# Four-layer image network on one NeuronCore: one scaled identity per state index for both channel halves, POOL units' decays in SBUF, 1024-wide silu and softplus, and an order planned over all instructions

## The chip, the core and the metric

The kernel runs on one core of a Trainium2 chip. The metric is the device time of one execution in microseconds (us). The engines are called PE (TensorE), DVE (VectorE), ACT (ScalarE), POOL (GpSimd) and SP (SyncE, which here only issues DMAs).

## The reference, cut to what matters

Thirty-two images of 128 channels and 32x32 pixels (1024 tokens) go through four layers, each with a group norm ahead of it and an addition behind it: a 3x3 convolution, a selective scan (Mamba) over the tokens in four directions, a coordinate attention with two small scans, and a simulated four-qubit circuit. Nearly all the time goes into the second:

```python
uc = silu(conv1d(u)); dt = softplus(dtr @ dt_proj_w.T + dt_proj_b); A = -exp(A_log)
def step(h, inp):                      # for each token, d in 256 channels, n in 16 states
    dA = exp(dt_t[..., None] * A)
    h = dA * h + (dt_t * u_t)[..., None] * B_t[:, None, :]
    y = einsum('bdn,bn->bd', h, C_t)
y = (ys + uc * Dp) * silu(z)           # v0..v3: as is, channels flipped, tokens flipped, both
```

## The kernel before, in words

For each image the second layer is cut into 128 **units**: 4 directions `d` x 2 channel halves `h` x 16 state indices `n`. Sixteen units in a row with one `d` and `h` are a pass. A unit works on 128 channels x 1024 tokens in f32:

- ACT computes its decay exp(dt * A_n) (L1160).
- Its input du * B_n (du is dt * u) is made in one of three ways, by the letter of the unit in the table `KINDS` (L48). **D**: PE spreads the row B_n over the partitions into a PSUM slot (L1659), DVE multiplies by du (L1455). **P**: a DMA of SP reads the row B_n from HBM, broadcast to 128 partitions, into `b_rows` (L861), and POOL multiplies (L966) into the unit's ring slot in SBUF. **Z**: ACT scales the turned (tokens by channels) du by B_n, one 128x128 chunk at a time (`zmul`, L1069), and PE turns the result back into a PSUM slot (`turn_z`, L1662).
- DVE runs the scan along the tokens (L1469) into the slot `u % 8` of `ring`. One operand of each scan is in PSUM: for D and Z the input, with the decay in the ring; for P the decay, with the input in the ring.
- For each pair of units POOL multiplies both ring slots at once by the broadcast rows C_n (L983, the "product"), which another DMA has brought into `c_rows` (L867).
- PE turns each product and adds it into `y_acc` in PSUM (`add_y`, L1667), which frees the ring slot. A P unit's input may be written once the unit 8 back has been added.

All other work (the norms, the convolutions, the projections, the last two layers of the image before, the front of the image after) is a list of `step`s that the planner `lay` (L468) puts between the units on each engine by costs, due times and a table of shifts, `SHIFTS`. In the program before, the units' own instructions keep a fixed order on each engine (`unit_programs`, L363), and side steps are inserted at places of it. On POOL that order is: inputs of the P units of the next pair, then the product of this pair. Each engine runs its instructions in order.

SP issues the row loads in one in-order queue, `load_pair(k)` (L851) for k = 0, 1, 2, ...: the B rows of the P units of pair k, each once the buffer is free, and then the C rows of pair k, once the product `CB_BUFS` pairs back is done:

```python
for u in (2 * k, 2 * k + 1):
    if kind_of(u) == "P":
        if j >= B_BUFS: sp.wait_ge(pool_input, j - B_BUFS + 1)
        sp.dma_start(b_rows[:, j % B_BUFS, :], ...)
sp.wait_ge(prod_ready, s * PAIRS + k - CB_BUFS + 1)
sp.dma_start(c_rows[:, b, :, :], ...)
```

With `CB_BUFS` = 4 the B rows of pair k stand behind the C rows of pair k-1, which wait for the product of pair k-5.

Of the kernel before, what the change touches and what calls it, by code (L numbers as in the profile page):

```python
# [35 lines left out]
BANK = 512  # L36
# [7 lines left out]
PASSES = DIRS * HALVES  # L44
UNITS = PASSES * NST
# [70 lines left out]

def norm(tag, after=()):
    b = ("norm", tag)
    return [step(("moment", tag, 0), "A", None, after), step(("moment", tag, 1), "A"), step(("group_mean", tag), "P", b),
            step(("group_neg", tag), "A", b), step(("group_eps", tag), "D", b), step(("group_rstd", tag), "G"),  # L120
            step(("group_shift", tag), "A"), step(("norm", tag), "A")]
# [15 lines left out]
def silu_pair(of, d, h, name, parts, after=()):  # L137

    key = lambda c: (of, d, h, c)
    steps = []  # L140
    for c in range(2):
        for k in parts:
            steps += [step((name, d, h, *k, c), "P", key(c), after if not steps else [])]
    return steps + [step(("silu", of, d, h, c), "A", key(c)) for c in range(2)]


def operands(d, first=False):

    steps = []
    for h in range(HALVES):  # L150
        steps += silu_pair("u", d, h, "conv_in", [(k,) for k in range(TAPS)])
    if d % 2:
        for h in range(HALVES):
            taken = [] if first and d == 1 else [("take", 2 + h if d == 3 else "before")]
            steps += silu_pair("z", d, h, "z", [()], taken)
# [8 lines left out]
def timestep(d, h):  # L164

    steps = []
    for c in range(2):
        b = ("dt", d, h, c)
        parts = [("part", d, 2, c)] if (d, h) != (0, 1) else []
        steps += [step(("dt_proj", d, h, c), "P", b, parts)]  # L170
        steps += [step((k, d, h, c), e, b) for k, e in (("dt_soft", "A"), ("dt_copy", "A"), ("dt_u", "D"))]
    return steps


def turn_du(d, h, last=None):

    steps = []
    for c in range(2):
        b = ("turn_du", d, h, c)
        after = [] if c or last is None else [("zmul", last, 1)]  # L180
        steps += [step(("turn_du", d, h, c), "P", b, after), step(("turned_du", d, h, c), "A", b)]
    return steps if "Z" in KINDS[HALVES * d + h] else []
# [11 lines left out]
def mix():  # L194

    steps = [step(("take", "before"), "D", None, [("sum", -1)])] + turn_y("before", 1, 1)
# [55 lines left out]
def set_up():  # L252
# [11 lines left out]
    for f in range(2):  # L264
        for h in range(HALVES):
# [13 lines left out]
SIDE_COST = {"conv_in": .9, "xproj": .9, "z": 1., "dt_proj": .42, "mix": .9, "conv0": .9, "nin": 1., "adjust": .9,  # L279
             "turn_y": .5, "turn_du": .5, "turned_du": .6, "turn_b": .6, "turned_b": .3, "zmul": 1.35, "rest": .3, "dtproj2": .9, "in2": 2., "spread2": .95, "mask2": 3.4, "xproj2": .9, "out2": .9, "unitary": .5,  # L280
             "post": 1.8, "group_mean": .7, "angles": 1.8, "gates": .5, "mlp1": .5, "mlp2": .5, "turn": .3, "squeeze": .3,
             "silu": .68, "cb_rows": .6, "part": .6, "dt_soft": .66, "dtsoft2": .3, "dtw": .3,
             "dt_copy": .6, "dt_u": .7, "turned_y": .6, "h1": .8, "relu2": .8,
             "squeeze_gelu": .4, "silu2": .8, "mlp_gelu": .3, "sine": .6, "decay2": .6, "moment": 1.25, "group_neg": .45, "group_shift": .25, "norm": 1.25,
             "add0": .75, "keep0": .9, "keep1": .9, "keep2": .9, "keep3": .9, "add1": .7, "over": .5, "over_copy": .6, "sums": 3.5, "taps2": 1.7, "tapsum2": 1.05, "dta2": 1.1, "input2": .7,
             "scan2": 1.25, "prod2": .7, "ysum2": 1.05, "outer_h": 1.25, "outer_w": 1.25, "times_x": .7, "add2": .7,
# [1516 lines left out]
```

## Time and profile before

| | us |
|---|---|
| median of 3 runs (13699.96 to 13713.61) | 13713.5 |
| the profiled execution | 13695.55 |
| its span in the trace | 13693.8 |

Line numbers below are those of the kernel before. In the rows "busy" is the time that an engine executes, "idle before, releaser" is the time that it stood still just ahead of an instruction and what ended it. "From issue to landing" is the time of a DMA from the start of its issue on SP until its data is there. PE records are doubled for f32 operands of a true matmul (two records a chunk), and not for turns.

### The profile page before, as it was taken

The page shows a single profiled execution, that of the slowest core. Times are in us where ns is not written, and L with a number is a line of the kernel's source. Part 1 is how long each engine was busy: PE and PEld are TensorE (multiplying, and loading weights), DVE is VectorE, ACT ScalarE, POOL GpSimd, SP SyncE. Part 2 cuts the span into 40 slices and gives each one's busy share as a digit, 9 for nine tenths or more (in the row PEclk, how much of TensorE's full clock was granted, in tenths as well). Part 3 has the DMA queues.
Part 4 walks back from the last instruction along what each step waited for, and adds up shares of the span by engine and source line. Part 5 has one row for each costly group of instructions (what it writes and reads, how often), then busy time and mean ns, then how long its engine had stood idle before and what let it go on. Part 6 is the DMA issues. An engine that isn't in the chain of part 4 may idle for free.

```text
span 13693.8 us, 182039 instructions
## 1 busy us (share of the span) xinstructions
PE 11889.6 (87%) x67228; PEld 8271.3 (60%) x67228; DVE 12477.9 (91%) x8406; ACT 11898.3 (87%) x18047; POOL 13045.4 (95%) x3978
## 2 busy tenths in 40 slices
PE   7888888888888888888888888888888888888886
PEld 4566666666666666566666566665666666666654
DVE  7899999999999999999999999999999999999985
ACT  6888888888888888888888888888888888888884
POOL 7999999999999999999999999999999999999995
PEclk8999999999999999999999999999999999999997
DMA  5566566656566666566665665655666656666552
GB/s 191 224 226 228 228 224 230 235 224 229 221 235 232 228 228 226 226 230 233 226 230 221 233 231 226 230 226 226 234 230 225 230 223 230 233 227 228 226 213 115
DMA packets 544698, 3067.83 MB, mean 224 GB/s; under 512 B 60378, under 2 KB 60474, under 8 KB 281538
## 3 DMA queue, kind: packets, MB, share of 16 engines
q1 hardware_dynamic: 543810, 3056.18, 59.1%
q8 instruction: 534, 8.75, 0.3%
q14 instruction: 354, 2.90, 0.1%
HBM read 2990.40 MB, written 48.76 MB: 222 GB/s over the span
## 4 chain that ended last, share of the span: by engine, by line
POOL 33%; PE 22%; issue 16%; ACT 13%; DVE 9%; DMA 4%; POOLq 0%; DVEq 0%; SPq 0%; ACTq 0%
POOL ring L983 24%; PE work L1481 10%; POOL ring L966 8%; PE y_acc L1496 7%; DVE ring L1469 6%; ACT ring L1160 3%; ACT L1000 3%; DMA cb_rows_scratch<-stack 2%; PE y_acc L1481 2%; DVE slot L1455 2%; PE slot L1496 1%; DMA b_rows<-cb_rows_scratch 1%; PE slot L1481 1%; ACT slot L1160 1%; ACT z_t L1069 1%
## 5 line engine op out<-in xcount | busy, mean ns | idle before, releaser
L983 POOL TENSOR_TENSOR ring<-ring,c_rows 128x2048 f32<-128x2048 f32 x2048 | 9297.0, 4548 | 392.6 <-DVE ring L1469 375.4
L1469 DVE TENSOR_TENSOR_SCAN ring<-ring,slot 128x1024 f32<-128x1024 f32 x2560 | 5817.8, 2280 | 218.7 <-PE slot L1496 82.3
L1496 PE MATMUL y_acc<-wk,ring 128*128 128x128 f32 x32768 | 4513.7, 284 | 671.7 <-POOL ring L983 656.5
L1496 PEld LDWEIGHTS y_acc<-wk,ring 128*128 128x128 f32 x32768 | 3984.0, 147 | 1506.1 <-POOL ring L983 850.8
L1469 DVE TENSOR_TENSOR_SCAN ring<-slot,ring 128x1024 f32<-128x1024 f32 x1536 | 3495.0, 2276 | 370.4 <-POOL ring L966 266.4
L966 POOL TENSOR_TENSOR ring<-du,b_rows 128x1024 f32<-128x1024 f32 x1536 | 3634.2, 2369 | 64.7 <-DMA b_rows<-cb_rows_scratch 53.3
L1160 ACT ACTIVATE ring<-dt,a_neg 128x1024 f32<-128x1024 f32 x2560 | 2846.2, 1139 | 19.6 <-PE y_acc L1496 9.8
L1000 ACT ACT_TABLE_LOAD x1883 | 2415.9, 1283 | 33.7
L1455 DVE TENSOR_TENSOR slot<-du,slot 128x1024 f32<-128x1024 f32 x1856 | 2246.1, 1210 | 73.5 <-PE slot L1481 71.4
L1481 PE MATMUL work<-h_new,fused 128*128 128x512 f32 x4096 | 1936.5, 603 | 8.6 <-DVE padded L1334 3.1
L1160 ACT ACTIVATE slot<-dt,a_neg 128x1024 f32<-128x1024 f32 x1536 | 1707.1, 1113 | 240.6 <-DVE ring L1469 230.6
L1069 ACT ACTIVATE z_t<-du_t,b_t 128x128 f32<-128x128 f32 x5632 | 1792.2, 389 | 33.0 <-PE slot L1496 10.2
L1481 PE MATMUL slot<-stack,sel 96*128 96x512 bf16 x3712 | 1200.5, 407 | 291.6 <-DVE ring L1469 284.2
L1481 PEld LDWEIGHTS work<-h_new,fused 128*128 128x128 f32 x4096 | 735.1, 193 | 630.5 <-issue 591.6
L1481 PE MATMUL work<-padded,wk 128*128 128x512 f32 (+1 forms) x1792 | 927.5, 622 | 53.0 <-ACT u_conv L1039 31.9
L1496 PE MATMUL slot<-wk,z_t 128*128 128x128 f32 x5632 | 778.4, 282 | 193.4 <-DVE ring L1469 176.3
L1496 PEld LDWEIGHTS slot<-wk,z_t 128*128 128x128 f32 x5632 | 648.1, 144 | 455.2 <-issue 372.8
L1481 PEld LDWEIGHTS slot<-stack,sel 96*128 96x128 bf16 x3712 | 320.3, 102 | 861.6 <-DVE ring L1469 506.8
L1050 ACT ACTIVATE stack<-work 32x512 bf16<-32x512 f32 x768 | 448.3, 584 | 313.7 <-PE work L1481 299.8
L1481 PE MATMUL work<-u_conv,wk 128*125 128x512 f32 x1024 | 515.0, 620 | 24.0 <-ACT yz L1078 20.6
L1481 PEld LDWEIGHTS y_acc<-diag_d,u_conv 128*128 128x128 f32 x4096 | 494.9, 192 | 60.3 <-issue 33.0
L1481 PE MATMUL y_acc<-diag_d,u_conv 128*128 128x128 f32 x4096 | 508.1, 277 | 0.0
(178 smaller groups left out, 9934.9 us busy)
## 6 DMA issues: line engine op xcount, KB each, us to landing
c_rows<-cb_rows_scratch SPq DMA_DIRECT2D x2048, 1024.0 KB, 4.7
b_rows<-cb_rows_scratch SPq DMA_DIRECT2D x1536, 512.0 KB, 5.6
x_next<-in_x SPq DMA_DIRECT2D x32, 512.0 KB, 5.6
x_new_scratch<-x_next SPq DMA_DIRECT2D x32, 512.0 KB, 7.8
h_old<-h_new SPq DMA_DIRECT2D x32, 512.0 KB, 7.9
x_old<-x_new_scratch SPq DMA_DIRECT2D x32, 512.0 KB, 10.1
out<-x_old SPq DMA_DIRECT2D x32, 512.0 KB, 7.9
cb_rows_scratch<-stack SPq DMA_DIRECT2D x128, 116.0 KB
```

Of the source, the lines that this page charges most:

```text
L966: pool.tensor_tensor(ring[:, u % RING, :], du[:, h, :], b_rows[:, j % B_BUFS, :], ALU.mult).then_inc(pool_input, 1)
L983: pool.tensor_tensor(pair, pair, c_rows[:, k % CB_BUFS, :, :], ALU.mult).then_inc(prod_ready, 1)
L1000: act.preload_act_table_set(name)
L1050: ins = act.activation(half(stack[r, d % 2, :], c), w[r, :], ACT.Copy)
L1069: ins = act.activation(z_t[:, turned % Z_BUFS, j * P:(j + 1) * P], du_t[:, j * P:(j + 1) * P], ACT.Copy, scale=b_t[:, d % 2, j * NST + n:j ...
L1160: act.activation(slot, dt[:, h, :], ACT.Exp, scale=a_neg[:, h * NST + n:h * NST + n + 1]).then_inc(decay_ready, 1)
L1455: dve.tensor_tensor(operand[u % 2], du[:, h, :], operand[u % 2], MUL).then_inc(input_ready, 1)
L1469: dve.tensor_tensor_scan(slot, a, b, 0.0, MUL, ADD).then_inc(scan_done, 1)
L1481: return pe.matmul(out_ap, w, x, start=start, stop=stop, skip_group_check=True)
L1496: ins = pe.matmul(chunk(out_t, j), chunk(x, j), kc("ident"), is_transpose=True, start=start and j % (BANK // P) == 0, stop=stop, skip_grou ...
```

## The change

`KINDS` has 58 D, 44 P and 26 Z units an image in place of 58, 48 and 22, and every Z stands at the same `n` in both halves of a direction. ACT now scales the **identity** by B_n once for both halves (13 times 8 chunks an image in place of 22 times 8), and `turn_z` is a true f32 matmul of du_t by that scaled identity. P units' decays go to `decays` in SBUF, so both operands of a P scan are in SBUF, and PSUM slots alternate over D and Z units alone. Silu, softplus, the copy of dt and dt * u take both banks at once (1024 wide). The halves are ordered 0, 1, 1, 0, 0, 1, 1, 0, so that `y_acc` carries over two passes at two places of an image: two takes and two identity additions fewer. Row sums for three of the four norms come from the additions' accumulators. `CB_BUFS` and `B_BUFS` go from 4 to 3. ACT issues the stores of the C and B rows. The planner orders all instructions of all engines itself, with other costs and a new `SHIFTS`; like the planner before, it has no term for the row loads except behind a store.

```diff
-KINDS = ('DPDPZDDDDPZPDPDZ', 'DPDZDPDZDPZPDPDP', 'DDDDDPZPDPPPZDDP', 'DPDPDPZZPPZZDPDP',
-         'DPZPPDPZDPPDZPDP', 'DDDPDPDDPDZZDDPD', 'DPDPDZZPDDDPDZDP', 'DPDPDPZDDPDPZPDP')
+KINDS = ('DPDPDZZDDPPZZDDP', 'DPDPDZZDPDPZZDDP', 'DPPDDPPDZDZDZDZP', 'DPDPDDDPZPZDZDZP',
+         'DPDZZPPDDDPPZDPP', 'DDPZZDDDPDPPZPDP', 'DPDDZDDPDPPDDZDP', 'DDDPZPPDPDPDDZDP')
-CB_BUFS = 4
-B_BUFS = 4
-Z_BUFS = 2
+CB_BUFS = 3
+B_BUFS = 3
+Z_BUFS = 4
+DECAY_BUFS = 2
...
-    (-413, 123, -1143, -1629, -1503, -1060, -1344, -1469, -1469, -2434, -2294, -1545, -1418, -1624, -1701, -489,
...
+def unit_flows(kind):
+    of = lambda *kinds: [u for u in range(UNITS) if kind_of(u) in kinds]
+    return {"D": [[("b", u) for u in of("D")], [("scan", u) for u in range(UNITS)]],
+            "G": [[("input", u) for u in of("P")], [("prod", u) for u in range(1, UNITS, 2)]],
...
     if k == "input":
-        return [(("sum", u - RING), 0)] * (u >= RING) + [(("dt_u", d, h, 1), 0)] * (u >= NST and first_of("P", u)) + rows
+        return [(("sum", u - RING), 0)] * (u >= RING) + [(("dt_u", d, h), 0)] * (u >= NST and first_of("P", u)) + rows
...
-                if k >= CB_BUFS or s > 0:
-                    sp.wait_ge(prod_ready, s * PAIRS + k - CB_BUFS + 1)
+                if loads >= CB_BUFS:
+                    sp.wait_ge(prod_ready, loads - CB_BUFS + 1)
...
-                    for j in range(4 * i, 4 * i + 4):
-                        ins = act.activation(z_t[:, turned % Z_BUFS, j * P:(j + 1) * P], du_t[:, j * P:(j + 1) * P], ACT.Copy,
-                                             scale=b_t[:, d % 2, j * NST + n:j * NST + n + 1])
+                    for j in range(CH // Z_STEPS * i, CH // Z_STEPS * (i + 1)):
+                        ins = act.activation(z_t[:, tile_of(u), j * P:(j + 1) * P], kc("ident"), ACT.Copy,
+                                             scale=b_turned(d, s)[:, j * NST + n:j * NST + n + 1])
...
-                        slot = operand[u % 2]
-                        if u >= 2 or s > 0:
-                            act.wait_ge(scan_done, s * UNITS + u - 1)
+                        slot = decays[:, (s * N_P + number("P", u)) % DECAY_BUFS, :]
...
-                    turn(operand[u % 2], z_t[:, (s * N_Z + number("Z", u)) % Z_BUFS, :], True, True).then_inc(z_turned, 1)
+                    for j in range(CH):
+                        ins = mm(chunk(slot_of(u, s), j), chunk(du_t, j), chunk(z_t[:, tile_of(u), :], j),
+                                 j % (BANK // P) == 0, True)
```

**POOL, the start of a middle image** (units 1, 3, 9, ... are P; `b_rows` rows are inputs, `c_rows` rows are products of pairs). Before:

```order
L966 TENSOR_TENSOR ring<-du,b_rows 128x1024 x2
L983 TENSOR_TENSOR ring<-ring,c_rows 128x2048 x3
L966 TENSOR_TENSOR ring<-du,b_rows 128x1024
L983 TENSOR_TENSOR ring<-ring,c_rows 128x2048
L966 TENSOR_TENSOR ring<-du,b_rows 128x1024
```

and now:

```order
L1100 TENSOR_TENSOR ring<-du,b_rows 128x1024 x2
L1109 TENSOR_TENSOR ring<-ring,c_rows 128x2048
L1100 TENSOR_TENSOR ring<-du,b_rows 128x1024
L1109 TENSOR_TENSOR ring<-ring,c_rows 128x2048 x2
L1100 TENSOR_TENSOR ring<-du,b_rows 128x1024
```

The input of unit 9, in pair 4, stood behind the products of pairs 0, 1 and 2, and stands behind that of pair 0 now. Counted over a middle image: before, 47 of 48 inputs had three products between the one that releases their B row and themselves, and one had four; now 7 of 44 inputs come behind that product with no other between, 24 have one between, 10 have two, and 3 have three.

**SP, the same place** (row loads with the semaphores that they wait for). Before:

```order
L861 DMA b_rows<-cb_rows_scratch 128x1024 [waits pool_input]
L867 DMA c_rows<-cb_rows_scratch 128x2048 [waits prod_ready] x3
L861 DMA b_rows<-cb_rows_scratch 128x1024 [waits pool_input]
L867 DMA c_rows<-cb_rows_scratch 128x2048 [waits prod_ready]
L861 DMA b_rows<-cb_rows_scratch 128x1024 [waits pool_input]
```

and now:

```order
L1004 DMA b_rows<-cb_rows_scratch 128x1024 [waits pool_input]
L1010 DMA c_rows<-cb_rows_scratch 128x2048 [waits prod_ready] x3
L1004 DMA b_rows<-cb_rows_scratch 128x1024 [waits pool_input]
L1010 DMA c_rows<-cb_rows_scratch 128x2048 [waits prod_ready]
L1004 DMA b_rows<-cb_rows_scratch 128x1024 [waits pool_input]
```

The queue reads the same: the B row of unit 9 stands behind the C rows of pairs 1 to 3. What moved is the product that the last of these waits for: with 4 buffers it was the last of the image before, with 3 it is that of pair 0.

## Rows read from the trace of the kernel before

**Rows 1.** The page's first lines: span, busy time of each engine.

```profile
span 13693.8 us, 182039 instructions
PE 11889.6 (87%) x67228; PEld 8271.3 (60%) x67228; DVE 12477.9 (91%) x8406; ACT 11898.3 (87%) x18047; POOL 13045.4 (95%) x3978
```

**Rows 2.** A window of 419 us in the middle: engines' busy us, PEclk, DMA share, GB/s.

```profile
1940.30:2359.30 419.00, 367.77 (x2105) 255.57 (x2104) 391.24 (x260) 372.97 (x567) 408.50 (x127) 0.96 0.62 229
```

**Rows 3.** An instruction that POOL runs once an image, from 1600 to 13100 us.

```profile
L929 POOL TENSOR_TENSOR m<-m x27: 444/450/503, 1940.3 to 12833.9; 128x128 f32<-128x128 f32 x27
```

**Rows 4.** POOL's waits in those 26 images: us in total, times, longest.

```profile
POOL ring L983 <- DVE ring L1469: 263.0, 259, 2.7
```

**Rows 5.** The costliest groups of POOL: busy us, mean ns, idle before and releaser.

```profile
L983 POOL TENSOR_TENSOR ring<-ring,c_rows 128x2048 f32<-128x2048 f32 x2048 | 9297.0, 4548 | 392.6 <-DVE ring L1469 375.4
L966 POOL TENSOR_TENSOR ring<-du,b_rows 128x1024 f32<-128x1024 f32 x1536 | 3634.2, 2369 | 64.7 <-DMA b_rows<-cb_rows_scratch 53.3
```

**Rows 6.** Timeline of POOL: start us, us.

```profile
13477.04 4.53 POOL L983 TENSOR_TENSOR ring<-ring,c_rows 128x2048 f32<-128x2048 f32 x1
13481.52 2.37 POOL L966 TENSOR_TENSOR ring<-du,b_rows 128x1024 f32<-128x1024 f32 x1
13483.84 4.54 POOL L983 TENSOR_TENSOR ring<-ring,c_rows 128x2048 f32<-128x2048 f32 x1
```

**Rows 7.** Timeline of POOL and SP's queue in the middle: start us, us.

```profile
5998.40 4.55 POOL L983 TENSOR_TENSOR ring<-ring,c_rows 128x2048 f32<-128x2048 f32 x1 [0.66 <-DVE ring L1469]
6002.99 0.32 SPq L867 DMA_DIRECT2D c_rows<-cb_rows_scratch  x1
6003.35 0.43 SPq L861 DMA_DIRECT2D b_rows<-cb_rows_scratch  x1
```

**Rows 8.** DMA issues, whole span, then two single loads: KB, median us to landing.

```profile
b_rows<-cb_rows_scratch SPq DMA_DIRECT2D x1536, 512.0 KB, 5.6
...
b_rows<-cb_rows_scratch SPq DMA_DIRECT2D x1, 512.0 KB, 5.1
...
b_rows<-cb_rows_scratch SPq DMA_DIRECT2D x1, 512.0 KB, 7.3
```

**Rows 9.** Timelines of SP and of POOL, the first image's first B row.

```profile
92.18 0.33 SPq L861 DMA_DIRECT2D b_rows<-cb_rows_scratch  x1
...
96.68 2.35 POOL L966 TENSOR_TENSOR ring<-du,b_rows 128x1024 f32<-128x1024 f32 x1 [50.35 <-DMA b_rows<-cb_rows_scratch]
```

**Rows 10.** Timeline of PE: a turn (x8), a true matmul of 8 chunks (x16).

```profile
6015.54 1.04 PE L1496 MATMUL slot<-wk,z_t 128*128 128x128 f32 x8
6016.42 1.13 PE L1481 MATMUL work<-wk,h_new 128*128 128x128 f32 x8
...
6041.58 1.95 PE L1481 MATMUL y_acc<-diag_d,u_conv 128*128 128x128 f32 x16
6043.36 1.04 PE L1496 MATMUL y_acc<-wk,ring 128*128 128x128 f32 x8
```

**Rows 11.** Groups of ACT, DVE and PE that the change touches: busy us, mean ns, idle.

```profile
L1000 ACT ACT_TABLE_LOAD x1883 | 2415.9, 1283 | 33.7
L1069 ACT ACTIVATE z_t<-du_t,b_t 128x128 f32<-128x128 f32 x5632 | 1792.2, 389 | 33.0 <-PE slot L1496 10.2
...
L1469 DVE TENSOR_TENSOR_SCAN ring<-slot,ring 128x1024 f32<-128x1024 f32 x1536 | 3495.0, 2276 | 370.4 <-POOL ring L966 266.4
...
L1282 DVE TENSOR_TENSOR du<-work,u_conv 128x512 f32<-128x512 f32 x512 | 346.9, 677 | 77.3 <-ACT dt L1058 77.3
L1286 DVE TENSOR_TENSOR yz<-y_acc,silu_z 128x1024 f32<-128x1024 f32 x128 | 155.2, 1213 | 149.9 <-PE y_acc L1496 149.4 <-ACT yz L1078 0.5
...
L1481 PE MATMUL y_acc<-yz,wk 128*128 128x512 f32 x512 | 247.3, 605 | 0.0
```

**Rows 12.** Timeline of the set-up: a POOL instruction over DVE's with two SBUF inputs.

```profile
14.23 0.55 POOL L925 TENSOR_TENSOR bnw<-bnw,neghalf 128x1 f32<-128x1 f32 x1 [11.51 <-DVE bnw L1214]
14.34 1.34 DVE L1188 SCALAR_TENSOR_TENSOR fused<-c_rows 128x256 f32<-128x256 f32 x3
```

More of the change, by code:

```diff
@@ L143, in silu_pair, with conv, gate_z, project @@
             steps += [step((name, d, h, *k, c), "P", key(c), after if not steps else [])]
-    return steps + [step(("silu", of, d, h, c), "A", key(c)) for c in range(2)]
-def operands(d, first=False):
-    steps = []
[L150 to L155, printed above, removed]
+    return steps + [step(("silu", of, d, h), "A", both(key(0), key(1)))]
+def conv(d, h):
+    return silu_pair("u", d, h, "conv_in", [(k,) for k in range(TAPS)])
+def gate_z(f, h, after=()):
+    return silu_pair("z", f, h, "z", [()], after)
+def project(d):
+    steps = []
     for c in range(2):
@@ L194, in mix @@
 def mix():
-    steps = [step(("take", "before"), "D", None, [("sum", -1)])] + turn_y("before", 1, 1)
+    steps = [step(("take", "before"), "D", None, [("sum", -1)])] + turn_y("before", 1, 0)
     for c in range(2):
@@ L276, in set_up @@
     return [[step(("zero",), "G")], weights, decays, scales, mixes, circuit]
[L279 to L286, printed above, removed]
-             "result": .75, "group_rstd": .55, "take": 1.2, "du2": .7, "zero": 2.5, "fuse": .43, "kron": 1.5, "gate": .17, "bn_rstd": .55, "m1": 2., "postw_mask": .35, "dterm2": .7, "dadd2": .7, "yz2": .7}
@@ L602, in image_streams @@
     takes = []
-    for p in range(PASSES - 1):
-        f, t, h = p // 4, p // 2 % 2, p % 2
-        after = [("sum", p * NST + NST - 1)]
-        if t == 0 and not first:
+    for p in TAKES:
+        f, h = p // 4, parts_of(p)[1]
+        after = [("sum", p * NST + NST - 1)] + ([("silu", "z", f, h)] if p % 4 else [])
+        if not first and p % 4 != 3:
             after += [(("post", 1) if h else ("angles",)) if f else ("mix", 4, 1)]
-        takes += [step(("take", p), "D" if t else "A", None, after)]
-        if t:
+        takes += [step(("take", p), "D" if p % 4 else "A", None, after)]
+        if p % 4:
             takes += turn_y("this", f, h)
@@ L635, in count @@
     def count(steps, e):
-        return sum(x[2] == e for x in steps)
+        return sum(x[1] == e and x[3] is not None for x in steps)
     def bases(kind, s):
@@ L647, in numbers @@
         n, out = dict.fromkeys("PADG", 0), {}
-        for x in steps:
-            n[x[2]] += 1
-            out[x[1]] = (x[2], n[x[2]])
+        for name, e, _, after in steps:
+            if after is not None:
+                n[e] += 1
+                out[name] = (e, n[e])
         return out
@@ L943, in step @@
                 ins.then_inc(side["G"], 1)
-            for _, name, e, _, after in before:
+            for name, e, _, after in before:
                 if e == "G":
@@ L986, in _ @@
             each_image(pool, image)
-            for _, name, e, _, after in finish:
+            for name, e, _, after in finish:
                 if e == "G":
@@ L1431, in _ @@
             dve.wait_ge(weights_in, 16 * 7)
-            for _, name, e, bank, after in before:
+            for name, e, bank, after in before:
                 if e == "D":
@@ L1633, in _ @@
             pe.wait_ge(weights_in, 16 * 7)
-            for _, name, e, bank, after in before:
+            for name, e, bank, after in before:
                 if e == "P":
@@ L1691, in image @@
-                side_steps(END["P"])
+                    turn(y_acc, ring[:, u % RING, :], starts, ends).then_inc(sum_done, 1)
+                for name, _, bank, after in order_of(plans[kind], "P"):
+                    if name[0] == "spread":
+                        spread_b(name[1])
+                    elif name[0] == "zturn":
+                        turn_z(name[1])
+                    elif name[0] == "sum":
+                        add_y(name[1])
+                    else:
+                        hold(pe, "P", base, of, after)
+                        step(name, image_of(name, s), bank_of[bank])
```

614 lines of the change are left out of this document (343 added, 271 removed), and 92 rows, old and new, of the table SHIFTS.

## The prediction

> **What bounds the kernel now.** I read the busy times first [rows 1]: POOL is busy for 95% of the span, DVE 91%, PE and ACT 87%. A window of one image in the middle says more [rows 2]: of 419.0 us POOL works 408.5, DVE 391.2, ACT 373.0, PE 367.8. That 419 us is the period: the instruction that POOL runs once an image goes from 1940.3 to 12833.9 us in 26 steps, which is 418.98 each [rows 3]. So POOL has 10.5 us to spare in an image. Its waits say what they are: 263.0 us in 26 images, 10.1 an image, go to products that wait for DVE's scans [rows 4]. Whatever changes POOL's time by x us an image changes the total by 32x; what the other engines save or pay counts only through a wait of POOL.
>
> POOL's work is 64 products and 48 inputs an image [rows 5]. By starts, a product takes 4.48 us and an input 2.32 [rows 6].
>
> **The change, part by part.**
>
> *Four P units fewer.* 4 x 2.32 = 9.3 us less POOL work an image. This is the whole gain on the engine that bounds.
>
> *Z units.* ACT scales 104 chunks an image in place of 176, at 1792.2 / 5632 = 0.318 us [rows 11]: -22.9 us of ACT. PE pays: a turn of 8 chunks takes 0.88 us from start to start, a true matmul of 8 chunks 1.78 [rows 10], so 22 x 0.88 becomes 26 x 1.78: +26.9. Two of four identity additions go: 247.3 / 32 / 2 = -3.9 [rows 11]. PE comes to 390.8 us an image, ACT to 350.
>
> *Wide silu, softplus, copy, dt * u; fewer table loads.* The program has 1471 table loads where there were 1883: 412 x 1.283 / 32 = -16.5 us of ACT [rows 11]. DVE's 512 half products of 0.677 us become 256; at 1.21 us, what the 1024-wide take takes [rows 11], that is -1.2 us. Both lie beside POOL's work and I cost them at nothing: the cover is POOL's period, and ACT and DVE stay under it.
>
> *Decays in SBUF, slots over D and Z alone.* DVE's scans of P units waited 266.4 us for POOL's inputs in all [rows 11]; scans that come sooner can only take from the 10.1 us of rows 4. In the other direction, both operands of 44 scans an image now come from SBUF. No scan of the trace does that. From below it costs nothing: the scan takes 2.276 us with the decay in PSUM. From above it costs POOL the whole scan, 44 x 2.28 = 100 us. I take nothing, since the one row that is near shows nothing, and keep the other end as a rival: in the set-up, POOL's L925 runs from 14.23 to 14.78, and DVE starts three instructions with two SBUF inputs at 14.34; they take 1.34 us, 0.45 each, with no gap, and POOL's is done in 0.55 [rows 12]. It reads one element a partition, so the row is weak.
>
> The Trainium skill, "SBUF — State Buffer", section "Who interferes with whom", speaks against this part: a DVE instruction with two SBUF inputs and a GpSimd one that reads SBUF exclude each other for the whole instruction. The rows of the set-up don't agree with it; by it the sum would be that of the second rival.
>
> *The B rows: three buffers and a free order.* Here the change loses what it wins. A P unit's B row is loaded behind the C rows of the pair before, in SP's one queue. With three C buffers those wait for the product of the pair four back. The row lands late: the product that starts at 5998.40 frees SP, which issues the C rows at 6002.99 and the B row at 6003.35 [rows 7], so 0.4 us after the product's end; the B row takes 5.6 us more by the median [rows 8]. The input can't start until 6.0 us after that product's end. Before, three products (13.4 us) lay between, and in the whole run POOL waited for B rows only at the start (53.3 us, rows 5). Now the order puts inputs up to there. I went through the 44 inputs of a middle image and added up the POOL work between the releasing product and the input: 2 inputs have nothing between (units 9 and 63), 4 have 2.3 us (another input), 9 have 4.5 us (a product), 2 have 5.0, and the rest 6.0 or more. The waits are 2 x 6.0 + 4 x 3.7 + 9 x 1.5 + 2 x 1.0 = 42.3 us; unit 38's row also waits for its buffer, freed 4.7 us before it is wanted, 0.9 more. A wait shelters the input behind it; walked through in order, with each wait moving all that follows, 39.6 us are left, in 18 inputs. The walk with 5.1 us from issue to landing, the quicker of the two single loads in rows 8, gives 31.6; with 6.0 it gives 46.4. The slower single load took 7.3, and a load into an idle queue, the first of all, 4.5 until POOL ran [rows 9], so no row shows one under 4.5.
>
> *What goes as POOL gets late.* The 10.1 us for scans: POOL now stands still 40 us an image elsewhere, and DVE, at 390 us of work, catches up meanwhile. All or none of it may go; I take 7, since the new waits are spread over the whole image but a scan also waits for a late input.
>
> *The stores from ACT, `x` loads, set-up and the last image's end* move by a few us in all: nothing.
>
> **The sum.** 419.0 - 9.3 + 39.6 - 7.0 = 442.3 us an image, 23.3 more than now; 32 x 23.3 = 746. On the profiled execution's 13695.6 that is 14441; the median of the runs shown lies 18 us higher, so 14460. PE at 390.8 and DVE at 390 have over 50 us to spare in that period. The ends: 419.0 - 9.3 + 31.6 - 10.5 = 430.8 gives 14090; 419.0 - 9.3 + 46.4 = 456.1 gives 14900.
>
> **The rivals.**
>
> *Faster: the loads are early enough.* If the B rows land before POOL wants them, only the first part is left: 419.0 - 9.3, and up to 5 us less waiting for scans, as ACT has 40 us less work and slots come free sooner. That is 13400 (13255 at best). It decides by the landing: at 4.1 us from issue, 4.5 from the product's end, the 9 inputs behind one product wait for nothing, 2 x 4.5 + 4 x 2.2 = 17.8 us are left, and with 9.3 and 7 off, the period is that of now. For it: the DMA engines are busy 62% of the time [rows 2], so a load might be quicker where the C rows ahead have landed. Against it: the C rows of 1 MB are issued 0.36 us ahead every time, and even the idle queue took 4.5. Chance 0.13, and 0.03 that it comes out within 0.2%, which is about what a measurement of this kernel can tell from no change.
>
> *Much slower: P scans and POOL exclude each other.* Each of the 44 scans of 2.28 us keeps POOL still, 100.3 us an image. Where it falls into POOL's waits for B rows it is free, so the period is between 442.3 + 100.3 - 39.6 = 503.0 and 542.6, and the time between 16400 and 17670, say 17000. For it: the kernel before has one operand in PSUM in every large DVE instruction beside POOL, even where ACT must write a second time for it. Against it: rows 12. It decides as soon as POOL and DVE can't both read; then products stretch beyond 4.54 us or P scans beyond 2.28. Chance 0.18.
>
> *The change doesn't do what it says* can't be on this engine: 1408 inputs are in the program where 1536 were.
>
> **How the numbers follow.** The forecast, 14460 with its own range of 14090 to 14900, has 0.64; the faster rival 0.13; no change 0.03; the exclusion 0.18; slower by another way, such as PE's sums freeing the ring too late at 390.8 us of work, 0.02. Slower by over 0.2% is then 0.84. The range must leave out no more than 0.2: it reaches from the faster rival, 13300, to 14900 and leaves the exclusion out.
>
> **What the profile would show.** POOL's inputs with B rows as what ended their wait, some 18 an image, 35 to 45 us an image in all, the longest near 6 us; POOL busy near 90%, with 1408 inputs of 2.37 us and products unchanged at 4.54; scans with both operands in SBUF at 2.28; the once-an-image instruction every 440 us; ACT under 80% of the span; B rows landing in 5 to 6 us. The forecast is wrong if POOL hardly waits for DMA, if a B row lands within 4.1 us of its issue, if the scans or products are longer than now, or if POOL waits for PE's sums instead.

## The result, and the profile after

The change takes 17046.0 us (median of 4 runs, 17015.5 to 17049.9) where the kernel before takes 13713.6: a ratio of 1.243, 95% interval 1.241 to 1.245. The forecast was 14460 and the range ended at 14900, so the time lies 2146 us beyond the range. It lies inside the second rival, the exclusion of P scans and POOL, which had 17000 and a chance of 0.18.

The page of the changed kernel, first lines (against [rows 1]), and a window of 533 us in its middle (against [rows 2]: the same columns, PE, PEld, DVE, ACT, POOL busy us, PEclk, DMA share, GB/s):

```profile
span 17045.9 us, 192114 instructions
PE 13574.0 (80%) x74844; PEld 9697.5 (57%) x74844; DVE 15134.9 (89%) x8150; ACT 10549.9 (62%) x14370; POOL 14465.0 (85%) x3850
```

```profile
6000.00:6533.00 533.00, 427.89 (x2379) 306.53 (x2379) 475.12 (x253) 339.12 (x463) 459.44 (x123) 0.90 0.48 178
```

POOL has 128 instructions fewer and is busy 1420 us longer; DVE has 256 fewer and is busy 2657 us longer. Both engines have fewer instructions, and those they have take longer. The groups say which (busy us, mean ns, idle before and releaser; against [rows 5] and [rows 11]):

```profile
L1109 POOL TENSOR_TENSOR ring<-ring,c_rows 128x2048 f32<-128x2048 f32 x2048 | 10198.4, 4992 | 802.6 <-DVE ring L1609 772.9 <-DMA b_rows<-cb_rows_scratch 18.1 <-PE y_acc L1645 11.5
L1609 DVE TENSOR_TENSOR_SCAN ring<-ring,slot 128x1024 f32<-128x1024 f32 x2688 | 6067.1, 2272 | 246.7 <-PE slot L1630 199.3 <-ACT ring L1299 18.9
L1609 DVE TENSOR_TENSOR_SCAN ring<-decays,ring 128x1024 f32<-128x1024 f32 x1408 | 5910.8, 4209 | 359.6 <-POOL ring L1100 358.7 <-issue 0.2
...
L1100 POOL TENSOR_TENSOR ring<-du,b_rows 128x1024 f32<-128x1024 f32 x1408 | 3951.7, 2812 | 1431.9 <-DMA b_rows<-cb_rows_scratch 1247.4 <-PE y_acc L1645 144.8 <-DVE ring L1609 38.1
...
L1134 ACT ACT_TABLE_LOAD x1470 | 1886.0, 1283 | 27.1
```

The scans with one input in a PSUM slot take 2.27 us, as before. Those with both in SBUF (`decays`, `ring`) take 4.21 us by the mean. POOL's product has gone from 4.548 to 4.992 us and its input from 2.369 to 2.812. The spread within a group is the better sign. This view of the tile `decays`, with minimum, median and maximum in ns, and that of an instruction which POOL runs once an image (0.45 us in [rows 3]) show it:

```profile
L1609 DVE TENSOR_TENSOR_SCAN ring<-decays,ring x1408: 2256/4274/6649, 101.6 to 16896.1; 128x1024 f32<-128x1024 f32 x176
```

```profile
L1068 POOL TENSOR_TENSOR m<-m x32: 452/2433/2445, 798.0 to 16962.7; 128x128 f32<-128x128 f32 x32
```

A scan takes between 2.26 us, its own time, and 6.65, its own time and most of a product's. The small POOL instruction takes 0.45 us or 2.43: 0.45 and most of a scan's 2.27. How one instruction comes to hold the other is read from the timeline of POOL and DVE at 6038 to 6062 us (start us, length us):

```profile
6037.98 4.53 POOL L1109 TENSOR_TENSOR ring<-ring,c_rows 128x2048 f32<-128x2048 f32 x1
...
6039.81 4.86 DVE L1609 TENSOR_TENSOR_SCAN ring<-decays,ring 128x1024 f32<-128x1024 f32 x1
6042.48 4.35 POOL L1100 TENSOR_TENSOR ring<-du,b_rows 128x1024 f32<-128x1024 f32 x1
6046.79 4.51 POOL L1109 TENSOR_TENSOR ring<-ring,c_rows 128x2048 f32<-128x2048 f32 x1
6046.83 2.27 DVE L1609 TENSOR_TENSOR_SCAN ring<-ring,slot 128x1024 f32<-128x1024 f32 x1
...
6053.60 4.54 POOL L1109 TENSOR_TENSOR ring<-ring,c_rows 128x2048 f32<-128x2048 f32 x1 [2.29 <-DVE ring L1609]
...
6056.88 3.40 DVE L1609 TENSOR_TENSOR_SCAN ring<-decays,ring 128x1024 f32<-128x1024 f32 x1
6058.09 2.44 POOL L1068 TENSOR_TENSOR m<-m 128x128 f32<-128x128 f32 x1
```

The product ends at 6042.51. The P scan starts at 6039.81, in the middle of it, and ends at 6044.67: that is 2.2 us, about one scan, after the product's end. The input starts at 6042.48 and ends at 6046.83, 2.2 us, about one input, after the scan's end. A product, a scan and an input stand one behind the other although two engines run them, and the wait is inside their durations; the views of waits don't list it. The next two lines are the control: a product and a scan with one input in a PSUM slot start together, at 6046.79 and 6046.83, and both take their own time, 4.51 and 2.27. The last three lines are like the first: product until 6058.14, scan until 6060.28, and only then the 0.45 us instruction, done at 6060.53.

The waits of POOL in 27 periods in the middle (us in total, times, longest; against [rows 4]):

```profile
POOL ring L1100 <- DMA b_rows<-cb_rows_scratch: 1068.6, 374, 8.3
POOL ring L1109 <- DVE ring L1609: 603.9, 310, 2.6
POOL ring L1100 <- PE y_acc L1645: 118.7, 97, 2.4
```

That is 39.6, 22.4 and 4.4 us an image. The once-an-image instruction runs from 1849.1 to 16042.2 us in 27 steps, a period of 525.7 where it was 419.0 [rows 3]. The period adds up: 64 products x 0.444 = 28.4 and 44 inputs x 0.443 = 19.5 longer; 39.6 for B rows; 12.3 more for scans; 4.4 for TensorE's sums; 2.0 in the small instruction; 9.3 less for four inputs: 96.9 of the 106.7. The rest was not added up.

### The profile page after: what moved, and what is told of

It reads as the page before. It is cut to its first block and busy times, and to the rows that moved or that the text cites. A ratio compares the mean times of both kernels' runs of the same rounds, so it can differ in the third digit from the quotient of the medians.

```text
span 17045.9 us, 192114 instructions
## 1 busy us (share of the span) xinstructions
PE 13574.0 (80%) x74844; PEld 9697.5 (57%) x74844; DVE 15134.9 (89%) x8150; ACT 10549.9 (62%) x14370; POOL 14465.0 (85%) x3850
## 5 line engine op out<-in xcount | busy, mean ns | idle before, releaser
L1109 POOL TENSOR_TENSOR ring<-ring,c_rows 128x2048 f32<-128x2048 f32 x2048 | 10198.4, 4992 | 802.6 <-DVE ring L1609 772.9
L1609 DVE TENSOR_TENSOR_SCAN ring<-ring,slot 128x1024 f32<-128x1024 f32 x2688 | 6067.1, 2272 | 246.7 <-PE slot L1630 199.3
L1609 DVE TENSOR_TENSOR_SCAN ring<-decays,ring 128x1024 f32<-128x1024 f32 x1408 | 5910.8, 4209 | 359.6 <-POOL ring L1100 358.7
L1100 POOL TENSOR_TENSOR ring<-du,b_rows 128x1024 f32<-128x1024 f32 x1408 | 3951.7, 2812 | 1431.9 <-DMA b_rows<-cb_rows_scratch 1247.4
L1299 ACT ACTIVATE decays<-dt,a_neg 128x1024 f32<-128x1024 f32 x1408 | 1602.6, 1142 | 1012.9 <-DVE ring L1609 1008.7
L1630 PEld LDWEIGHTS slot<-z_t,du_t 128*128 128x128 f32 x13312 | 1773.4, 213 | 472.2 <-issue 340.5
L1630 PE MATMUL slot<-z_t,du_t 128*128 128x128 f32 x13312 | 1863.0, 300 | 224.0 <-DVE ring L1609 217.7
L1206 ACT ACTIVATE z_t<-wk,b_t 128x128 f32<-128x128 f32 x3328 | 1144.9, 392 | 31.1
L1196 ACT ACTIVATE du_t<-work 128x512 f32<-128x512 f32 x512 | 304.3, 594 | 512.9 <-PE work L1645 509.4
L1630 PEld LDWEIGHTS work<-padded,wk 128*128 128x128 f32 (+1 forms) x1792 | 341.9, 210 | 410.1 <-issue 318.6
```

The costliest lines, as they stand in the source:

```text
L1100: pool.tensor_tensor(ring[:, u % RING, :], du[:, pass_of(d, h) % 2, :], b_rows[:, j % B_BUFS, :], ALU.mult).then_inc(pool_input, 1)
L1109: pool.tensor_tensor(pair, pair, c_rows[:, loads % CB_BUFS, :, :], ALU.mult).then_inc(prod_ready, 1)
L1196: ins = act.activation(half(du_t, c), w, ACT.Copy)
L1206: ins = act.activation(z_t[:, tile_of(u), j * P:(j + 1) * P], kc("ident"), ACT.Copy, scale=b_turned(d, s)[:, j * NST + n:j * NST + n + 1])
L1299: act.activation(slot, dt[:, pass_of(d, h) % 2, :], ACT.Exp, scale=a_neg[:, h * NST + n:h * NST + n + 1]).then_inc(decay_ready, 1)
L1609: dve.tensor_tensor_scan(slot, a, b, 0.0, MUL, ADD).then_inc(scan_done, 1)
```

## The experiments

Each kernel ran beside the kernel before on the same chip, which took 13698 to 13706 us by the median. "e3" and the like are the first letters of the labels. e1 has 4 runs, e7 has 10, e8 has 2, and e2, e3, e4, e5, e6 and e9 have one each; with one run, differences of less than some 40 us (0.3%) are not read.

**e1: the kernel before with three buffers of C rows.**

```diff
-CB_BUFS = 4
+CB_BUFS = 3
...
-                if k >= CB_BUFS or s > 0:
-                    sp.wait_ge(prod_ready, s * PAIRS + k - CB_BUFS + 1)
+                if loads >= CB_BUFS:
+                    sp.wait_ge(prod_ready, loads - CB_BUFS + 1)
```

The three buffers are counted on over the images, and three scratch places of the set-up move, since they lay in the fourth.

> The kernel before with three C buffers in place of four, its order unchanged. Both mechanisms' theory: each input still has two products (9 us) between the one that now releases its B row and itself, more than the 6.0 us that a row needs, so POOL waits for no B row and the time is that of before within 0.2%: 13685 to 13740. Rival (three buffers are too few by themselves, whatever the order): POOL waits for B or C rows, 2 us or more an image, over 13770.

Measured: 13792.0 us, ratio 1.0067 (1.005 to 1.0084), 93 us more. The theory of no waits missed, and the rival holds (over 13770, and 2 us or more an image of waits for rows). POOL's waits, whole run:

```profile
POOL ring L967 <- DMA b_rows<-cb_rows_scratch: 53.6, 3, 50.3
POOL ring L967 <- DVE ring L1472: 46.8, 18, 2.8
POOL ring L967 <- issue: 37.4, 15, 3.1
```

The start's 50 us were there before. The two lines under it, 84 us in 33 inputs, are new, up to 3.1 us each, about one an image. They name a scan or nothing, and no line names a DMA; the timeline says that they are late rows. Three of the 33 start at 4219.76, 6335.27 and 6758.58, and SP issued a B row 4.40, 4.30 and 4.28 us ahead of each, after some 10 us in which it had issued no row. So three buffers cost 0.7% by themselves.

**e2: e1, and the P units' decays in SBUF.**

```diff
+        decays = sb("decays", [P, 2, TOK])
-        a, b = operand[u % 2], slot
+        a, b = decays[:, (s * N_P + number("P", u)) % 2, :], slot
```

> The run above with one more edit: the decays of the 48 P units an image go to two buffers in SBUF, with the same waits and the same order. Exclusion theory: 1536 scans of 2.28 us each keep POOL still, 3502 us, less what falls into POOL's 336 us of idle time: 16700 to 17250; P scans stretch to 4 us or more by the mean, products beyond 4.6. Rival (no exclusion; the change's slowness is the B rows' waits or PE): scans stay at 2.28, time 13690 to 13760. Rival (ports are shared by access, not locked): P scans and products stretch by a part, 14000 to 15500.

Measured: 16893.0 us, 3101 more than e1, 96.9 us an image, inside the range of the exclusion theory; both rivals are out. Order, inputs, products and side work are those of e1.

```profile
L986 POOL TENSOR_TENSOR ring<-ring,c_rows 128x2048 f32<-128x2048 f32 x2048 | 9486.2, 4633 | 1462.9 <-DVE ring L1473 1432.2 <-PE y_acc L1500 26.4 <-DMA b_rows<-cb_rows_scratch 1.4
L1473 DVE TENSOR_TENSOR_SCAN ring<-decays,ring 128x1024 f32<-128x1024 f32 x1536 | 6972.7, 4541 | 187.0 <-POOL ring L968 142.5 <-ACT decays L1163 34.2 <-ACT ring L1163 0.6
...
L968 POOL TENSOR_TENSOR ring<-du,b_rows 128x1024 f32<-128x1024 f32 x1536 | 5091.6, 3317 | 139.0 <-DMA b_rows<-cb_rows_scratch 56.5 <-DVE du L1285 56.0 <-issue 21.9
```

This one edit alone makes the kernel before nearly as slow as the whole change. The upper bound of the prediction's rule, every P scan keeps POOL still for its length, is here 48 x 2.28 = 109 us an image; 89% of it came. It comes in two shapes: POOL's instructions last longer (busy 14988.9 us where [rows 1] has 13045.4; 1457 of these 1944 us are in the inputs, 189 in the products, the rest in small instructions), and POOL waits for scans that themselves waited (1432 us where [rows 5] has 375).

**e3: the change, B rows issued a pair earlier.** The B rows of pair k + 1 are issued ahead of the C rows of pair k, which wait for a product.

```diff
-        load_b(k, s); wait(product k - CB_BUFS); load_c(k, s)
+        load_b(k + 1, s); wait(product k - CB_BUFS); load_c(k, s)
```

> The changed kernel with the B rows of pair k+1 issued ahead of the C rows of pair k; order and all else as in the change. Walked through the order, POOL's waits for B rows fall from 39.6 to 1.4 us an image. Theory of two mechanisms that overlap: POOL's waits for B rows gave P scans a free time, so of the 1247 us only a part comes back, 200 to 900: 16150 to 16850. If they simply added: 15800. If the B rows were all of it: 13400. If they cost nothing beside the exclusion: 17000 to 17060.

Measured: 16478.0 us, 568 less than the change, in the range of the theory that the two mechanisms overlap. POOL's waits:

```profile
POOL ring L1119 <- DVE ring L1619: 918.7, 481, 7.9
POOL ring L1110 <- PE y_acc L1655: 386.6, 245, 4.7
POOL ring L1110 <- DMA b_rows<-cb_rows_scratch: 150.6, 33, 50.8
POOL ring L1119 <- DMA c_rows<-cb_rows_scratch: 131.2, 30, 5.2
```

1097 us of waits for B rows went. Half of it reached the time, the other half came back: as waits for scans (+146), for sums (+242), for C rows (+131), and in longer inputs (2.905 us for 2.812). The P scans still take 4.16 us.

**e4: the change, decays back in the PSUM slots, planned anew with the change's offsets.** The wait of each slot is again on the scan two units back, and the planner knows it.

```diff
-        slot = decays[:, (s * N_P + number("P", u)) % DECAY_BUFS, :]
+        slot = operand[u % 2]
-        scanned(earlier("DZ", u, 2))
+        scanned(u - 2)
```

> The changed kernel with the decays of P units back in the PSUM slots, which alternate over all units again, and the order planned by the same costs and shifts with that one constraint; B rows as in the change (by the walk 41.5 us of waits an image, 39.6 in the change). Theory of two mechanisms: no scan has two SBUF operands, so scans are 2.28 and products 4.55, and what is left is the forecast: 14460, between 14090 and 14900. Rival (PE's 23 us more work an image or the free order costs as well): over 14900. Rival (the B rows' waits are absorbed by others): under 13900.

Measured: 17612.4 us, slower than the change. The theory of two mechanisms missed. By its number the first rival holds, that something else costs as well (over 14900), but the trial had changed a second thing. Groups and POOL's and ACT's waits:

```profile
L1109 POOL TENSOR_TENSOR ring<-ring,c_rows 128x2048 f32<-128x2048 f32 x2048 | 9245.2, 4531 | 948.8 <-DVE ring L1609 940.8 <-DMA b_rows<-cb_rows_scratch 2.3
...
L1609 DVE TENSOR_TENSOR_SCAN ring<-slot,ring 128x1024 f32<-128x1024 f32 x1408 | 3189.8, 2273 | 560.0 <-POOL ring L1100 277.7 <-ACT slot L1299 274.3 <-ACT ring L1299 2.2
```

```profile
POOL ring L1100 <- DMA b_rows<-cb_rows_scratch: 1726.3, 679, 52.3
POOL ring L1109 <- DVE ring L1609: 940.8, 468, 15.4
POOL gn L1066 <- DVE gn L1419: 874.7, 90, 26.6
...
ACT slot L1299 <- DVE ring L1609: 1941.4, 646, 18.3
```

Scans are back at 2.27 us and products at 4.53: the exclusion is gone, and POOL is busy for 12767.8 us. But POOL now waits, for B rows and for scans, and ACT's decays wait 1941 us for a slot behind scans. I take the cause to be the order, which no run of this kernel alone shows. The offsets of the order were made for slots that only D and Z units use; with two slots for all units the same offsets give a bad order (494.8 us an image by the planner's own count, 412.8 for the change). An experiment that takes back one part of a planned kernel has to plan again in full. e8 does that; e5 goes round it.

**e5: the change, each P scan replaced by two reductions.** Order, waits, buffers and places in memory stay as they are; what the kernel leaves out is the recurrence of the 44 P units.

```diff
-        dve.tensor_tensor_scan(slot, a, b, 0.0, MUL, ADD).then_inc(scan_done, 1)
+        dve.tensor_reduce(seen[:, n : n + 1], a, AX.X, ADD)
+        dve.tensor_reduce(seen[:, n + 1 : n + 2], b, AX.X, ADD).then_inc(scan_done, 1)
```

> Left out: the recurrence of the 44 P units an image; in place of each P scan VectorE makes two reductions over 1024 columns (one over the decays, one over the ring slot), which have one SBUF input each. Order, waits for rows, buffers and all of POOL's work stay as in the change. Two ports of the same data, one operation after the other: estimated 2.2 to 2.6 us for the pair, as the scan's 2.28 alone. Theory A (the shared exclusion between a VectorE scan with both inputs in SBUF and POOL's products and inputs makes the change slow, and nothing else much does): P work 2.2 to 2.6 us, products 4.5 us, inputs 2.3 us as in the trace before; the waits of POOL for B rows stay at 39 to 47 us an image, and the time is 14090 to 14900, near 14460, as the forecast had it with this exclusion left out. Theory B (the SBUF traffic of the decays itself, not the pair of SBUF operands, or the order, is what costs): products and inputs stay above 4.9 and 2.7 us, and the time above 15500.

Measured: 15047.4 us, 1999 less than the change.

```profile
L1110 POOL TENSOR_TENSOR ring<-ring,c_rows 128x2048 f32<-128x2048 f32 x2048 | 9267.2, 4544 | 164.7 <-DVE seen L1611 111.9 <-DVE ring L1615 48.5 <-PE y_acc L1651 1.2
...
L1101 POOL TENSOR_TENSOR ring<-du,b_rows 128x1024 f32<-128x1024 f32 x1408 | 3326.9, 2367 | 1851.2 <-DMA b_rows<-cb_rows_scratch 1582.6 <-PE y_acc L1651 213.6 <-issue 23.5
...
L1611 DVE TENSOR_REDUCE seen<-ring 128x1 f32<-128x1024 f32 x1408 | 1701.9, 1209 | 0.0
L1610 DVE TENSOR_REDUCE seen<-decays 128x1 f32<-128x1024 f32 x1408 | 1696.5, 1205 | 454.8 <-POOL ring L1101 431.1 <-ACT ring L1300 21.5
```

The same operands are read from the same places, one an instruction, and POOL's instructions are as before: 4.544 and 2.367 us, with 1.21 us for each reduction. So it is not the SBUF traffic of the decays and not the order that stretches the instructions. e2 kept the scan and moved its operand, e5 keeps the operands and splits the scan; what the two leave is two SBUF inputs in one VectorE instruction. DVE's time stays comparable (2.41 us for a pair, 2.28 for a scan). The time is neither theory's: above the 14900 of A, under the 15500 of B; the durations are A's. What A missed is the size of the rest: the waits for B rows are 1582.6 us, 47.8 an image without the start's 52, and those for sums 6.7.

**e6: e5, B rows issued a pair earlier**, as in e3.

> The kernel with the two reductions in place of each P scan (the recurrence of the 44 P units an image is left out), and the B rows of the next pair issued ahead of the C rows of this one. Theory A (row waits and exclusion are the two costs, and they overlap): POOL's waits for B rows fall from about 40 to under 6 us an image, and the time to 13300 to 13700, the change's gain from four fewer P inputs with nothing against it. With the change itself (17046) and it with B rows ahead (16478) this makes a square: 568 us gained by the rows with the exclusion there, 800 to 1300 without it. Rival (other engines of the changed kernel hold it once POOL is free: wider ScalarE work, TensorE's scaled identities, the scans' DVE load): waits for B rows gone, but POOL waits for DVE or PE instead, and the time stays at 13800 to 14300.

Measured: 14152.5 us, 895 less than e5 (the step that theory A gave as 800 to 1300) and still 455 above the kernel before, where A had 13300 to 13700. POOL's waits:

```profile
POOL ring L1111 <- PE y_acc L1661: 405.0, 196, 5.4
POOL ring L1120 <- DMA c_rows<-cb_rows_scratch: 263.0, 62, 8.0
POOL ring L1111 <- DMA b_rows<-cb_rows_scratch: 250.3, 92, 51.9
POOL ring L1120 <- DVE seen L1621: 107.1, 171, 2.4
```

The rival's range was right, 13800 to 14300: POOL is only 90% busy and waits for PE's sums; it waits for rows as well, which the rival had as gone. With the change, e3 and e5 this is a square:

| | P scans with two SBUF inputs | without |
|---|---|---|
| B rows as in the change | 17046 | 15047 |
| B rows a pair earlier | 16478 | 14152 |

The exclusion costs 1999 or 2326 us, as far as two reductions (2.41 us) stand for a scan (2.28); the late rows cost 568 or 895. The two overlap by 327 us: a scan that keeps POOL still costs nothing where POOL stands waiting for a row.

**e9: e6, with the Z units' true products replaced by transpositions.** What the kernel leaves out besides is the multiplication by B in the Z units.

```diff
-        ins = mm(chunk(slot_of(u, s), j), chunk(du_t, j), chunk(z_t[:, tile_of(u), :], j), ...)
+        ins = turn(slot_of(u, s), du_t, True, True)
```

> As the kernel with two reductions in place of each P scan and with B rows ahead (14152), and besides the matrix product of each Z unit with the scaled identity is replaced by the transposition of du that the kernel before makes there (about 0.9 us in place of 1.8; left out: the multiplication by B in the Z units, and the recurrence of the P units). Theory PE (the Z units' true products load TensorE, so that sums come later, ring slots come free later, and POOL and ScalarE wait for them: 405 us of POOL's and 1074 us of ScalarE's waits for y_acc in that trace): TensorE is some 700 us less busy, POOL's waits for y_acc fall under 150 us and the time to 13650 to 13900. Rival (what is left over is the row loads with three buffers, 250 us for B and 263 us for C rows, and an order made for other costs): POOL's waits for y_acc turn into waits for rows or scans, and the time stays above 14000.

Measured: 14148.9 us, no difference. Windows from 2000 to 12000 us, of e6 and of e9 (PE's busy time first):

```profile
2000.00:6000.00 4000.00, 3621.97 (x21453) 2615.09 (x21454) 3586.59 (x2706) 3009.20 (x4133) 3665.61 (x1104) 0.95 0.57 215
6000.00:12000.00 6000.00, 5430.72 (x32218) 3927.06 (x32217) 5372.92 (x4042) 4513.66 (x6185) 5503.71 (x1652) 0.95 0.57 215
```

```profile
2000.00:6000.00 4000.00, 3501.15 (x19518) 2437.50 (x19517) 3577.23 (x2703) 3010.16 (x4132) 3663.72 (x1105) 0.92 0.58 215
6000.00:12000.00 6000.00, 5254.26 (x29347) 3672.08 (x29348) 5357.09 (x4036) 4514.23 (x6180) 5496.18 (x1651) 0.92 0.58 215
```

Theory PE falls. The edit takes 816 us of TensorE's Z work away (1783 to 967), but TensorE's busy time falls by 414 only, its mean granted clock goes from 0.95 to 0.92, and the sums' matmuls take 289 ns where they took 285. POOL's waits for sums rise from 405 to 455 us. So taking this load off TensorE doesn't bring the sums earlier, and the Z units' true products are not what keeps e6 above the kernel before. The order and the three C buffers are left as candidates. They were not taken apart, and this stays open.

**e7: the kernel before with B rows a pair earlier**, a try for a faster kernel.

> The kernel before with one thing changed: within a direction, the B rows of the next pair are issued ahead of the C rows of this one (four buffers of each, as before). Theory: POOL's 263 us of waits for B rows in the trace before come from the place of the B-row load behind a C-row load that waits for a product; moved ahead they go, down to the 50 us at the start, and as POOL bounds the kernel the time falls by 120 to 210 us, to 13490 to 13580 (less than the wait, since some of it turns into waits for VectorE). Rival: the B rows then collide with the C rows on the DMA engines or hold the C-row load behind a wait for an input, POOL waits for C rows instead, and the time stays within 0.2% of 13700.

Measured: 13707.2 us against 13705.7, ratio 1.0001 (0.9991 to 1.0011): the same. The rival's number holds, but not its reason, for POOL waits for no C row. The expectation rested on a misreading. The 263 us of [rows 4] are waits for DVE's scans, and [rows 5] has 53 us for B rows, all at the start. The trace of e7 shows the same two:

```profile
POOL ring L991 <- DVE ring L1477: 385.8, 334, 10.8
...
POOL ring L974 <- DMA b_rows<-cb_rows_scratch: 50.5, 1, 50.5
```

There was no row wait to take away, and the new place of the loads costs nothing. In a line of waits, read the releaser before the number.

**e8: the change with decays in the slots, a fourth C buffer, B rows earlier, and an order searched for it.** The planner also gets the time from a freed row buffer to the next row in it, and its offsets are searched anew.

```diff
-CB_BUFS = 3
+CB_BUFS = 4
-        decays = sb("decays", [P, DECAY_BUFS, TOK])
+        return [(("input", v), ROW_IN)] * (v >= 0) + ...
-    (33, -66, -75, -172, 65, -36, -31, -17, -144, -92, -57, -85, -22, -31, -121, -53, -217, -133, -102, -55, -73,
...
+    (172, -351, -453, 1490, 337, 220, 1296, 1110, 665, 1547, 1553, 2077, 2537, 2222, 1329, 2618, 581, -411, -1096, ...
```

> All of the change but the P units' decays in SBUF: scaled identities shared by the halves, wide silu and softplus, the free order, 44 P inputs an image; the decays stand in the PSUM slots again, the space goes to a fourth buffer of C rows, B rows are issued a pair ahead, and the offsets of the order are searched anew for these waits (by the planner's own count an image comes to 423.7, where the change comes to 412.8, the kernel before to 433.3 with other costs, and the same edit with the change's offsets to 494.8, which ran at about 541 us an image). Theory A (the SBUF decays are what makes the change slow, and the order of the earlier trial what made it 17612): scans 2.28, products 4.53, inputs 2.36 us, under 10 us an image of waits for rows, and 13900 to 14700. Beating the kernel before (13700) would need an image under 419 us, which four fewer inputs alone would allow; I expect it not to. Rival (the rest of the change has a large cost of its own, in TensorE's true products or in the wide banks): over 15000.

Measured: 14420.6 us, ratio to the kernel before 1.0525 (1.0494 to 1.0555), and 2625 us less than the change, as theory A had it (13900 to 14700). Groups, and POOL's waits:

```profile
L1574 DVE TENSOR_TENSOR_SCAN ring<-slot,ring 128x1024 f32<-128x1024 f32 x1408 | 3174.6, 2269 | 198.7 <-POOL ring L1065 174.9 <-ACT slot L1264 15.4 <-ACT ring L1264 7.8
```

```profile
POOL ring L1074 <- DVE ring L1574: 833.4, 481, 12.4
POOL ring L1065 <- PE y_acc L1610: 436.3, 240, 5.1
POOL m L1042 <- DVE m L1433: 128.5, 32, 15.1
...
POOL ring L1065 <- DMA b_rows<-cb_rows_scratch: 51.0, 1, 51.0
```

The rest of the change is in it but for the three C buffers and the place of the B rows. POOL is busy for 12761.8 us (13045.4 in [rows 1]) and never waits for a row after the start, yet it waits 833 us for scans where the kernel before waits 375. My reading is that the decays in SBUF buy a freer order: without them the two slots tie ACT, TensorE and DVE together, and the gain of four inputs is given back. No run separates this from the quality of the order, so "the rest of the change loses 5%" is shown for this order only. No kernel of this study beats the kernel before.

## Why the prediction was wrong

**What bounds the kernel** held for the kernel before. In the change it is no longer POOL alone: POOL is busy for 85% of the span and DVE for 89%, and each has waits for the other inside its busy time. The account of 525.7 us above goes by POOL's instructions and waits.

**Four P units fewer**: 12780.7 us of POOL work in e5, 13045.4 before, a difference of 265 us or 8.3 an image, where the step had 9.3. Right.

**Z units, wide silu and softplus**: 1470 table loads (the step had 1471), ACT at 62% of the span, and POOL waits for ACT for 30.4 us at the start and not again, as before. TensorE's load went up as worked out (12686 us busy in e6 where [rows 1] has 11890, 24.9 an image for the 23.0 of the step), and e9 shows that taking the Z part away again brings nothing. Right.

**Decays in SBUF** is the step that failed. "I take nothing, since the one row that is near shows nothing" took the lower end, 0, between 0 and 100 us an image. Measured: 96.9 us an image for 48 scans (e2 against e1), 62.5 for 44 in the change itself (the change against e5), where the late rows shelter some, and 72.7 with the rows early (e3 against e6). The row it rested on, [rows 12], has a POOL instruction of 0.55 us with one element a partition that starts 0.11 us ahead of DVE's. DVE's first instruction there took 425 ns (the 0.45 of the prediction is a third of the 1.34 us of three, with the steps between them), and the eight of its line, seven of them clear of that POOL instruction, take 419 to 425: nothing was held. The row has neither of the cases that cost, a long POOL instruction that starts first, or a POOL instruction that starts behind a long DVE one. In the second, even one of this size is held: the once-a-norm instruction of the same shape takes 0.55 us alone and up to 2.55 in e2:

```profile
L929 POOL TENSOR_TENSOR gn<-gn,neghalf x128: 537/548/2552, 19.3 to 16868.4; 128x1 f32<-128x1 f32 x128
```

The prediction called its row weak and let it decide. No other row of the trace before could help: not one large DVE instruction there had two SBUF inputs beside a busy POOL, as the prediction says itself. One of its signs of being wrong, scans or products longer than now, is what came. The Trainium skill, "SBUF — State Buffer", section "Who interferes with whom", had told of an exclusive lock for the whole instruction; by this rule, the trace of the change agrees, with 2.27 us scans that take up to 6.65 and products of 4.548 that take 4.992 by the mean. Between a rule that named this case and one row of another order and size, the value had to be near the rule's.

**The B rows** were predicted at 39.6 us an image in 18 inputs (31.6 to 46.4). The trace of the change has 39.6, in 14. That agreement is luck. In e5, where the forecast's own premise holds, the waits are 47.8 us. The walk through the order kept scans and sums out, and took 5.6 us for every landing; the median landing in e5 is 5.7, so the scans and sums that the walk left out are the likelier source of its error, which no run separates. A landing can also be quicker than the prediction's least of 4.5 us: in e1 three inputs run 4.3 to 4.4 us after the issue of a B row. In the change the exclusion hides part: POOL works longer between two inputs, so the rows are less late.

**What goes as POOL gets late** was 7 us less waiting for scans. In the change these waits grew by 12.3, as the scans are later. In e5 they are nearly gone, 160 us in the run (111.9 + 48.5) for 375: 6.7 us an image less, as said.

**The sum.** For the change without exclusion the forecast gives 14460. Of the two kernels that stand for it, e5 takes 15047, 587 us more, of which 262 are B rows (8.2 an image) and 214 waits for sums, which had 0.02 as a rival and nothing in the sum; e8, which has its rows early and another order, takes 14421. Even without the exclusion the sum would have been too low for this order; e5 lies 147 us beyond the range.

**The rivals.** The exclusion's frame, 503.0 to 542.6 us an image, holds the 525.7 measured, and its 17000 is 46 us off. The faster rival needed early rows and nothing else; e6 has the first and still takes 14152, not 13400, since POOL then waits for sums (12.7 us an image) and C rows (8.2). So the faster rival had too much at 0.13, and the exclusion far too little at 0.18: it was weighed by the row of the set-up.

## What to carry to other kernels

Before an operand of a VectorE instruction moves from PSUM to SBUF, count its SBUF inputs: if it gets two and GpSimd reads SBUF beside it, charge the full duration of both instructions, one after the other, and look for cover only afterwards. A row that shows no interference counts only if its instructions are long and it has both orders of start; and the views of waits here show none of this kind, while the minimum, median and maximum of a duration do. If a part of a planned kernel is taken back as a test, plan again for it, or replace the costly instruction by one that keeps every wait.

## What the runs showed of the hardware

- Two SBUF inputs in a scan and a POOL instruction that reads SBUF run one behind the other, in these traces, whichever started first: scans of 2.27 us take up to 6.65 (e2 up to 6.68), a POOL instruction of 0.45 us takes 2.43. A scan with one input in PSUM takes 2.25 to 2.29 us in the same trace, beside products too. Two reductions over the same operands, one SBUF input each, do nothing of the kind (1.21 us each, products 4.544). Whether it is POOL's reads or its writes that collide was not tried.
- Two costs on the same engine don't add: the second edit takes 895 us away after the first (1999), but 568 alone, as the waits lie on top of each other.
- TensorE with less to do was granted a lower clock: a mean of 0.92 in place of 0.95 of 2.4 GHz (e9 and e6, one run each), which lies between its two levels of 1.2 and 2.4, after 816 us of matmuls had been taken out, and half of what was taken out came back as longer matmuls. In e2, where TensorE was busy for only 78% of the stretch from 2000 to 12000 us, the mean is 0.87.
- The landing time of rows doesn't follow the load here: a B row takes 5.6 us from issue by the median in the kernel before and in the change, at 59% and 47% of the DMA engines' time over the run. The longest median, 6.2 us, is that of e4, which has the lowest share, 45%; all others are 5.5 to 5.7.
